# A language-model tower on one core: twelve shared groups ahead of the experts instead of eight, their input read from DRAM, and the own tokens' numbers worked out late

## What is computed

```python
table = where(is_num[:, None], sin(num_value[:, None] / 1000.0 * arange(1, 129)), weight)   # 12500 x 128
h = table[x]                                                  # 128 x 128 tokens, D = 128
# attention: 8 heads of 64, over each sequence; LN is a layer norm without weights
q, k, v = LN(h) @ Wq, LN(h) @ Wkv                              # split into heads
dots = q @ k.T * scale[h]; dots = where(eye, -1e-9, dots)
attn = mix_post(softmax(mix_pre(dots)))                       # 8x8 mixes over the heads
h = h + (attn @ v) @ Wout + bout
# experts: a shared MLP for all tokens, and two banks of 8 experts, top 1, 1280 places each
x2 = LN(h)
y = gelu(x2 @ Ws1 + bs1) @ Ws2 + bs2                          # FF = 512
y = y + bank(x2, Wr_sp, W1_sp, W2_sp) + bank(x2, Wr_fq, W1_fq, W2_fq)
out = h + y
# bank: expert = argmax(softmax(x2 @ Wr + br)); a token beyond place 1280 of its expert adds 0;
#       otherwise gate * (gelu(x2 @ W1[e] + b1[e]) @ W2[e] + b2[e])
```

## Time and profile before

| | |
|---|---|
| median of 3 runs | 1506.09 us (1505.55 to 1506.47) |
| profiled execution: its own time, its span | 1516.0 us, 1514.3 us |
| busy share TensorE, VectorE, ScalarE, GpSimd | 97%, 69%, 76%, 63% |
| mean granted TensorE clock | 0.997 of full speed |
| setup / attention / experts / shared stage, by the trace | 0 to 64.2 / to 1052 / to 1333 / to 1514.3 us |

### The profile page before, as it was taken

How to read it: one execution, slowest core, us unless ns; L and a number is a source line. 1 busy time by engine, 2 the same in 40 slices (tenths; PEclk the granted TensorE clock), 3 DMA queues, 4 the chain that set the end, 5 groups by cost and what they waited for, 6 DMA issues and landing times. The chain is left out here.

```text
span 1514.3 us, 33889 instructions
## 1 busy us (share of the span) xinstructions
PE 1465.3 (97%) x11160; PEld 1339.9 (88%) x11160; DVE 1047.0 (69%) x2811; ACT 1146.8 (76%) x3477; POOL 959.1 (63%) x991
## 2 busy tenths in 40 slices
PE   5789999999999999999999999988999999999999
PEld 2469888888888988889888898877999999999999
DVE  7887788788777887778887787763344333356665
ACT  5589888888888888888888888865555555555555
POOL 7175567888788888788878877664677566510000
PEclk9999999999999999999999999999999999999999
DMA  7324511211211111111111111022244234456665
GB/s 237 132 73 163 164 38 49 69 48 42 60 38 39 55 42 36 35 56 34 36 56 34 37 38 48 26 60 67 69 116 106 70 71 109 120 158 190 189 184 146
DMA packets 171503, 126.48 MB, mean 84 GB/s; under 512 B 30309, under 2 KB 154959, under 8 KB 171330
## 3 DMA queue, kind: packets, MB, share of 16 engines
q1 hardware_dynamic: 153794, 104.15, 23.3%
q0 software_dynamic: 17536, 20.17, 4.8%
HBM read 61.64 MB, written 78.66 MB: 93 GB/s over the span
## 5 line engine op out<-in xcount | busy, mean ns | idle before, releaser
L1129 ACT ACTIVATE expd<-masked,nmax 128x128 f32<-128x128 f32 x1024 | 396.0, 393 | 0.3 <-DVE nmax L1282 0.3
L925 POOL TENSOR_TENSOR prob<-expd,rtotal 128x1024 f32<-128x1024 f32 x128 | 243.5, 1902 | 117.3 <-DVE rtotal L1251 115.8
L1265 DVE COPY_PREDICATED masked<-off_diag,ps_s 128x1024 f32<-128x1024 int32 x128 | 175.0, 1367 | 164.3 <-PE ps_s L1018 164.3
L1062 PE MATMUL ps_o<-u,probT 128*128 128x128 f32 x2048 | 249.0, 275 | 0.0
L1062 PEld LDWEIGHTS ps_o<-u,probT 128*128 128x128 f32 x2048 | 238.9, 191 | 0.0
L1129 ACT ACTIVATION_READ_ACCUMULATOR expd<-masked,nmax 128x1 f32 x1024 | 197.0, 192 | 0.0
L1138 ACT ACTIVATE u<-ps_ut 128x1024 f32<-128x1024 f32 x128 | 131.4, 1026 | 66.3 <-PE ps_ut L1073 66.3
L1227 DVE TENSOR_TENSOR w_lo<-ps_w,w_hi 128x512 fp32r<-128x512 f32 x256 | 164.3, 681 | 0.9 <-ACT w_hi L1167 0.9
L1167 ACT ACTIVATE w_hi<-ps_w 128x512 fp32r<-128x512 f32 x256 | 146.1, 595 | 15.7 <-PE ps_w L1048 9.3
L1158 ACT ACTIVATE probT<-ps_ut 128x1024 f32<-128x1024 f32 x128 | 131.4, 1027 | 33.9 <-PE ps_ut L1030 27.5
L1046 PE MATMUL ps_w<-xT_hi,M_hi 128*128 128x256 f32 x512 | 154.1, 301 | 3.0 <-DVE xT_lo L1221 2.2
(11 more groups left out here) (261 smaller groups left out, 3824.9 us busy)
## 6 DMA issues: line engine op xcount, KB each, us to landing
turned<-x2T SPq DMA_DIRECT2D x32, 256.0 KB, 2.2
answers_sp<-zeros SPq DMA_DIRECT2D x16, 512.0 KB, 4.3
answers_fq<-zeros SPq DMA_DIRECT2D x16, 512.0 KB, 3.8
xT<-turned SPq DMA_DIRECT2D x56, 128.0 KB, 2.3
sh_back<-answers_sp SPq DMA_DIRECT2D x56, 128.0 KB, 2.4
sh_back<-answers_fq SPq DMA_DIRECT2D x56, 128.0 KB, 2.5
out<-res SPq DMA_DIRECT2D x56, 128.0 KB, 2.1
h_sb<-in_L_tok_weight SPq DMA_DIRECT2D x12, 512.0 KB, 5.9
```

The source lines that it names most:

```text
L925: nc.gpsimd.tensor_tensor(prob[k % 2][:, :].rearrange("p (g j) -> p g j", g=H), expd[k % 2][:, :].rearrange("p (g j) -> p g j", g=H), rtot ...
L1062: mm = nc.tensor.matmul(ps_o[:, 0:D], probT[k % 2][:, g * N:(g + 1) * N], u[k % 2][:, g * D:(g + 1) * D], start=(g == 0), stop=(g == H - 1))
L1129: ins = nc.scalar.activation(expd[(k - 1) % 2][:, g * N:(g + 1) * N], masked[(k - 1) % 2][:, g * N:(g + 1) * N], ACT.Exp, bias=nmax[(k - 1 ...
L1265: nc.vector.copy_predicated(masked[k % 2][:, :].rearrange("p (g j) -> p g j", g=H), off_diag[:, :].unsqueeze(1).to_broadcast([P, H, N]), p ...
```

## The change

Setup: VectorE makes all thousandths at once (`slice(0, VS)`) into `part`; `numbers` now holds the plain number and the flag, so that `kept` is written before the weights are loaded, and the own tokens' thousandths are made from the gathered plain numbers behind `reduce(5)`. The turns (`turn_b` and its like) go from VectorE to GpSimd. On GpSimd the own numbers are gathered ahead of the head masks, two and two own rows behind them, and the two fills of `masked` go from ScalarE to GpSimd, behind the products. On TensorE `turn` and `coefficients` come a step later, and `product` n in steps 6 to 12 instead of 5 to 12, two in the last. `WARM` is 6 instead of 13.

Attention: `HEAD` is 12. A group's xT comes by DMA from `turned` into `x1` or `expd[0]` (`load_head`, `head_x`), so `norm2`, `head_norm` and the turn into `ps_w` go; up uses `ps_s` and `ps_w` by turns (`up`); the three schedules are new. Shared stage: 52 groups; the head rows are summed a group of 256 rows at a time, every second step from step 1.

```diff
-HEAD = 8
+HEAD = 12
...
-WARM = 13
+WARM = 6
...
+            link.inc(nc.gpsimd.tensor_scalar(turn_b, row_f[:, :], TURN_HI, 0.0, ALU.mult, ALU.add))
+            link.inc(nc.gpsimd.tensor_scalar(turn_lo, row_f[:, :], TURN_LO, 0.0, ALU.mult, ALU.add))
+            link(nc.gpsimd.tensor_scalar(turn_hi.bitcast(F32R), row_f[:, :], TURN_HI, 0.0, ALU.mult, ALU.add))
+            link(nc.gpsimd.tensor_tensor(turn_b, turn_b, turn_hi, ALU.subtract))
+            link(nc.gpsimd.tensor_tensor(turn_lo, turn_lo, turn_b, ALU.add))
+            link(nc.gpsimd.tensor_tensor(turn_b, turn_hi, turn_lo, ALU.subtract))
+            pool.wait_ge(S["link"], 1)
+            link(nc.gpsimd.tensor_tensor(turn_b, turn_b, is_hi[:, :].to_broadcast([KR, D]), ALU.mult))
+            nc.gpsimd.tensor_tensor(turn_b, turn_b, turn_lo, ALU.add).then_inc(S["turn"], 1)
...
+            pool.wait_ge(S["ids0"], 16)
+            pool.wait_ge(S["kept"], 32)
+            for t in range(OWN):
+                own_number(t)
...
-            pool.wait_ge(S["kept"], 32)
-            for t in range(OWN):
-                own_number(t)
-            pool.wait_ge(S["coef_out"], 2)
-            pool.wait_ge(S["wT_out"], 1)
-            for c in range(2 * HC):
-                mix(c)
+            for t in range(2):
+                own_row(t)
             for t, value in ((C.power, -0.5), (C.ones, 1.0), (C.tri, 1.0), (C.carry, 0.0), (C.chosen, 0.0), (C.var, 1.0)):
                 link.inc(nc.gpsimd.memset(t[:, :], value))
             for m in (*C.mv1, *C.mv2):
                 link.inc(nc.gpsimd.memset(m[:, :, :], 1.0))
             made["mv1"] = link.n
+            for t in range(2, OWN):
+                own_row(t)
+            pool.wait_ge(S["coef_out"], 2)
+            pool.wait_ge(S["wT_out"], 1)
+            for c in range(2 * HC):
+                mix(c)
+            for k in range(2):
+                link.inc(nc.gpsimd.tensor_copy(masked[k][:, :].rearrange("p (g j) -> p g j", g=H),
+                                               diag[:, :].unsqueeze(2).to_broadcast([P, H, N])))
...
+            sp.wait_ge(S["numbers"], 2)
+            sp.dma_start(kept[0:P * VR, :].rearrange("(p r) c -> p (r c)", p=P),
+                         numbers[:, 0:VR, :].rearrange("p r c -> p (r c)")).then_inc(S["kept"], 16)
+            sp.dma_start(kept[P * VR:VOCAB, :], numbers[0:REST, VR, :]).then_inc(S["kept"], 16)
...
-                if 5 <= c:
+                for n in {6: (0,), 7: (1,), 8: (2,), 9: (3,), 10: (4,), 11: (5,), 12: (6, 7)}.get(c, ()):
...
+            link(nc.vector.tensor_copy(numbers[:, 0:VS, 0], num_i[:, :]))
+            thousandths(slice(0, VS), flags=True)
+            halves(slice(0, CHUNKS - 1), VC)
...
+                    thousandths(slice(VS, VX))
...
-        AFTER = {129: (0,), 130: (1,), 131: (2,), 132: (3,), 136: (4,), 138: (5,), 139: range(6, HEAD + 2)}
-        BEHIND = {129: (0,), 130: (1,), 131: (2,), 134: (3,), 137: (4,), 139: range(5, HEAD + 2)}
-        BESIDE = {129: (0,), 131: (1,), 132: (2,), 133: (3,), 136: (4,), 137: (5,), 139: range(6, HEAD + 2)}
-        names = ("head_w", "head_made", "head_turned", "head_xhi", "head_xlo", "head_up", "head_gelu",
+        AFTER = {129: (1,), 130: (2,), 131: (3,), 132: (4,), 135: (5,), 136: (6,), 137: (7,), 139: range(8, HEAD + 2)}
+        BEHIND = {128: (0,), 129: (1,), 130: (2,), 131: (3,), 132: (4,), 135: (5,), 137: (6,), 139: range(7, HEAD + 2)}
+        BESIDE = {128: (0,), 129: (1,), 130: (2,), 131: (3,), 132: (4,), 135: (5,), 136: (6,), 137: (7,), 139: range(8, HEAD + 2)}
...
+        def up(m, f):
+
+            return hidden(ps_s, f) if m % 2 == 0 else ps_w[f // 2][:, f % 2 * GROUP:(f % 2 + 1) * GROUP]
+
+        def head_x(n):
+
+            return expd[0][:, n % 4 * GROUP:(n % 4 + 1) * GROUP] if n % 4 > 1 else x1[n % 4][:, :]
...
+            def load_head(groups):
+                for n in groups:
+                    need(sp, S["head_xlo"], n - 3)
+                    sp.dma_start(head_x(n), turned[n // 2, :, n % 2 * GROUP:(n % 2 + 1) * GROUP]).then_inc(s_head[n % 4], 16)
...
+                        sp.wait_ge(s_kept[k], 16 * (HEAD // 4 + 1))
+                    sp.wait_ge(S["x_turned"], GROUPS)
+                    load_head(range(2))
+                    sp.wait_ge(S["normed"], TILES - 1)
+                    load_head(range(2, 4))
+                if q == QUADS - 2:
+                    load_head(range(4, 8))
+            load_head(range(8, HEAD))
...
-                    if n < HEAD:
-                        pe.wait_ge(S["head_made"], n + 1)
-                        need(pe, S["head_xlo"], n - 1)
-                        need(pe, S["w_lo"], GROUPS * 4)
-                        for b in range(2):
-                            mm = nc.tensor.transpose(ps_w[n % 2][:, b * P:(b + 1) * P], x1[n % 2][:, b * D:(b + 1) * D], ident[:, :])
-                        mm.then_inc(S["head_turned"], 1)
                     if 0 <= n - 1 < HEAD:
                         m = n - 1
                         pe.wait_ge(S["head_xlo"], m + 1)
                         pe.wait_ge(S["copied"], TILES)
-                        need(pe, S["head_gelu"], m)
+                        pe.wait_ge(S["w_lo"], GROUPS * 4)
+                        need(pe, S["head_gelu"], m - 1)
                         for f in range(FC):
-                            h = hidden(ps_s, f)
+                            h = up(m, f)
...
-                        act.wait_ge(S["head_turned"], n + 1)
+                        act.wait_ge(s_head[n % 4], (n // 4 + 1) * 16)
                         need(act, S["head_up"], n - 3)
-                        nc.scalar.activation(xT_hi[:, n % 4, :], ps_w[n % 2][:, 0:GROUP],
+                        nc.scalar.activation(xT_hi[:, n % 4, :], head_x(n),
...
-                        head_norm(0)
                         link.wait()
                         link.inc(nc.vector.tensor_tensor(ws1_lo, ws1, ws1_hi.bitcast(F32), ALU.subtract))
-                    if n + 1 < HEAD:
-                        head_norm(n + 1)
                     if n < HEAD:
                         dve.wait_ge(S["head_xhi"], n + 1)
-                        nc.vector.tensor_tensor(xT_lo[:, n % 4, :], ps_w[n % 2][:, 0:GROUP],
+                        nc.vector.tensor_tensor(xT_lo[:, n % 4, :], head_x(n),
...
-        HEADS_FROM = 4
-
-        def head_tile(i, k):
-
-            n = (k - HEADS_FROM) // 3
-            return (n, n) if (k - HEADS_FROM) % 3 == 0 and 0 <= n < 2 * HEAD else None
+        HEADS_FROM = 1
+
+        def head_group(k):
+
+            n = (k - HEADS_FROM) // 2
+            return n if (k - HEADS_FROM) % 2 == 0 and 0 <= n < HEAD else None
...
+                n = head_group(k + 2)
+                if n is not None:
                     need(sp, S["one_out"], n - 1)
                     for b in range(BANKS):
-                        sp.dma_start(one_back[b][n % 2][:, :], answers[b][bass.ds(t * P, P), :]).then_inc(s_one[n % 2], 16)
...
+                n = head_group(k)
+                if n is not None:
                     dve.wait_ge(s_one[n % 2], (n // 2 + 1) * 32)
+                    need(dve, S["one_out"], n)
+                    for b in range(2):
+                        t = 2 * n + b
+                        ins = nc.vector.scalar_tensor_tensor(one_part[:, b, :], one_back[0][n % 2][:, b, :], gates[:, 2 * t:2 * t + 1],
+                                                             h_sb[:, t * D:(t + 1) * D], ALU.mult, ALU.add)
+                    ins.then_inc(S["one_part"], 1)
+                n = head_group(k - 1)
+                if n is not None:
+                    dve.wait_ge(S["one_part"], n + 1)
                     need(dve, s_one_put[n % 2], n // 2 * 16)
-                    need(dve, S["one_out"], n)
-                    nc.vector.scalar_tensor_tensor(one_part[:, :], one_back[0][n % 2][:, :], gates[:, bass.ds(t * 2, 1)],
-                                                   h_sb[:, bass.ds(t * D, D)], ALU.mult, ALU.add).then_inc(S["one_part"], 1)
-                    dve.wait_ge(S["one_part"], n + 1)
-                    nc.vector.scalar_tensor_tensor(one_out[n % 2][:, :], one_back[1][n % 2][:, :], gates[:, bass.ds(t * 2 + 1, 1)],
-                                                   one_part[:, :], ALU.mult, ALU.add).then_inc(S["one_out"], 1)
+                    for b in range(2):
+                        t = 2 * n + b
+                        ins = nc.vector.scalar_tensor_tensor(one_out[n % 2][:, b, :], one_back[1][n % 2][:, b, :], gates[:, 2 * t + 1:2 * t + 2],
+                                                             one_part[:, b, :], ALU.mult, ALU.add)
+                    ins.then_inc(S["one_out"], 1)
```

(11 more changed lines are left out.)

105 lines of the change are left out of this document (34 added, 71 removed).

## The result

The changed kernel takes 1527.73 us (median of 4 runs, 1524.25 to 1527.98) against 1505.82 us for the kernel before beside it (1504.11 to 1506.47): ratio 1.0142, 95% interval 1.0124 to 1.016. It is 1.4% slower, 12.4 us more than predicted and outside the range. Its profiled execution took 1527.67 us with a span of 1525.9. (One timed execution of the kernel before, beside later runs, took 2663.67 us at a granted clock of 0.76; it is in none of the comparisons.)

What follows compares the result with a forecast made beforehand. It took TensorE, busy 97% of the span, as the bound, and the end of GpSimd's run in the setup. Setup +4.9, tail +15.4, shared -12.6 and +0.5, clock +1: +9.2 on 1506.1, 1515.3 us, range 1502 to 1521.

Steps and rivals of the forecast that it cites:

- from the profiled execution to the median: Last step: the profiled execution lay 9.9 us above the runs' median, 1506.1; that difference was carried over to the forecast.
- (a): Setup: GpSimd's eight products begin at 22 to 25.5 us, taken as 24, so no shift.
- (b): Setup: the two fills of masked on GpSimd behind the products keep VectorE blocked 2.1 us more (0 to 3.8).
- (c): Setup: own numbers worked out behind reduce(5), eight chained operations of 0.19 to 0.2 us; TensorE resumes 1.6 us later.
- (d): Setup: all eight TensorE products now stand behind the wait for the own numbers; one more behind the stall, 1.9 us.
- (e): Setup: WARM 13 to 6 drops 14 matmuls, 1.6 us, of which only 0.65 us comes off.
- Tail: Attention's tail: work +12.1 us, idle 11.2 against 7.9, with waits of 2.3, 2.7, 1.7, 2.8; +15.4 us (11 to 17).
- Shared: Last stage: four fewer groups at 3.16 us, -12.6, and +0.5 for the wait at its start.
- Clock: Tail: gaps of 2.3 to 2.8 us may lower the granted clock, 0 to 5 us; +1 taken.
- the second place would fill the gaps: Rival: tail idle falls to 3.5 us, products begin 1.5 us sooner, fills and numbers find cover; 1499.7 us, chance 0.15.
- one had the tail filled too: Rival: the tail fills but the setup loses; +0.5, 1506.6 us, chance 0.13.
- the other the setup even: Rival: tail as walked, fills don't block VectorE and products begin early; +4.3, 1510.4 us, chance 0.15.

Runs made afterwards that it cites:

- gather_ahead: The kernel before with the last of GpSimd's four own-number gathers moved behind the products' two waits, directly ahead of the products; 1516.67 us, 1.0076.
- setup_only: The kernel before with the changed kernel's setup and WARM 6; 1522.25 us, 1.0117.
- fills_act: setup_only with the two fills of masked back on ScalarE; 1522.06 us, 1.0121.
- copy_first: setup_only with a GpSimd wait for the fourth reduction added ahead of its products, which had nothing to wait for; 1523.39 us, 1.012.
- both: The changed kernel with the wait of copy_first and the four tail steps moved as in tail_order; 1515.67 us, 1.0072.
- early_only: setup_only with VectorE's small operations on the own numbers moved ahead of the products, no idle added; 1517.68 us, 1.0093.
- tail_order: tail_only with four tail steps moved: gelu(0) and gelu(1) later, down(2)'s sum behind the normalizing, xT_lo(7) ahead of the last router step; 1497.43 us, 0.9952.
- tail_only: The changed kernel with the setup of the kernel before and WARM 13; 1509.88 us, 1.0042.
- mixes_late: The kernel before with a GpSimd wait for ScalarE's third sine added ahead of its eight products; 1506.4 us, 1.0009.
- rows_first: Changed setup on the old tail and stages, GpSimd's four row gathers ahead of its wait for kept, own numbers early; 1505.46 us, 1.0013.
- best: The changed kernel with the setup of rows_first and the tail of tail_order; 1496.5 us, 0.9955.
- memset_ahead: The kernel before with six memsets moved from behind GpSimd's products to directly ahead of them, behind their waits; 1504.19 us, 1.0003.
- idle_ahead: setup_only with a GpSimd wait for ScalarE's copy of wkT added ahead of the products, leaving idle time there; 1519.5 us, 1.0091.
- tail_act: tail_only with only ScalarE's part of the reordering, gelu(0) behind u(126) and gelu(1) behind u(127); 1503.19 us, 0.9983.

## Why the prediction was wrong

- **The step that failed is the last one: from the profiled execution to the median.** "That execution is 9.9 us above the median of the runs; the difference goes to the median." It took the 9.9 us as an offset that every profiled execution has over the runs. They were a thing in that one profile: the lock-out of VectorE, which gather_ahead prices at 11.5 us. Most executions of the kernel before don't have it; the changed setup has it in all six profiles in which its gathers of rows stand directly ahead of the products (after, setup_only, fills_act, copy_first, both, early_only). So the earlier trace rows, on which the setup was priced, is not the course that the median of before goes: against the usual course the setup costs 17.1 us (setup_only), not 4.9. Against the profile the forecast was +9.2 (1525.2 us), and 1527.67 was measured: 2.5 us off. The other 9.9 us of the miss are this step. The prediction had the number in hand (an execution 0.66% over runs that agreed within 0.06%) and the row (a copy of 15.58 us where its neighbours take 1.29) and didn't join them.
- **The 2.5 us are in part luck.** Against the profile of the rows the first turn came 5.9 us later (4.9 predicted). Behind it stand 1.8 us more until the first scores and 1.3 in the attention loop (922.2 us against 920.9), both priced at nothing, and the tail's 16.6 (15.4, and 1 for the clock). The experts, priced at nothing too, took 2.2 us less: their first 20 us had a granted clock of 0.83 before and 1.00 after, which is 3.4 us, while the wait for their rows was 1.2 us instead of 0.6. That gain, which no term foresaw, covers about half of what the setup, the start and the loop cost beyond the forecast.
- **(a) Products at 24.** They began at 25.57, 1.6 us late and 0.07 past the bounds of 22 to 25.5. `kept` landed at 11.45 and not by 10.5, and a mask on GpSimd took 1.52 us against a copy. More important than when: what stands ahead of them. That was on no list.
- **(b) Fills.** 2.01 us for two, and VectorE was held for both, as said. The Trainium skill ("SBUF — State Buffer", section "Who interferes with whom"), by which a GpSimd instruction that reads blocks a two-input VectorE instruction, agrees: 17.94 us with the fills (setup_only), 15.97 without (fills_act).
- **(c), (d), (e).** From the end of the fills to TensorE's resumption 4.67 us (47.06 less 42.39), where before had 3.33: +1.3 against 1.6. From there to the first turn 23.75 against 22.8: +0.95 against 1.9 - 0.65 = 1.25. All right in the locked course. In the other course (c) is 14.8 us, and the prediction had no rival for it.
- **Tail.** The four waits came as walked: 2.31, 2.66, 1.54 and 2.56 against 2.3, 2.7, 1.7 and 2.8. From last scores to last down +16.6 us against +15.4 (75.5 less 58.9); the clock was 0.91 from 1025 to 1045 us in it, so the +1 for the clock belongs here.
- **Shared.** From its first matmul to the end 169.4 us against 181.3: -11.9, predicted -12.1.
- **Clock.** +1 was taken for the tail. tail_order shows 3.7 beyond the waits (12.5 less 8.8), and the attention's start lost 1.8 us more than in the profile of before (9.0 us from first turn to first scores, against 7.2; clock 0.66 from 70 to 80 us). In after's own tail the clock was 0.96 over the first 38 us, 1.5 us lost, with the same waits that came with 5.0 in tail_only.
- **Rivals.** That the second place would fill the gaps fell, since they are the order of the program, and for the reason given; moving four steps fills most of them. The other two fell as well: one had the tail filled too, the other the setup even, and it costs 5.9 us even against the locked course.

## What to carry to other kernels

Where the profiled execution lies apart from the timed ones by more than they lie apart from each other, look for the rows that make it so before anything is priced: here the offset was a course that the other runs don't take. Two waits that end together hide each other: the table above has 2.8 and 4.6 us for either and 17.5 for both, so a cause is not cleared because its removal alone brings little. In a chain of engines near its end, give each engine what another waits for ahead of what fills (u before gelu, the normalizing before a sum), and count the cover of the longest latency (router to rows) in units of work before moving any away.

## What the runs showed of the hardware

- GpSimd's eight products and VectorE's two-input copies take turns, product by product (20.2 us for eight instead of 14.86, a copy 1.3 to 3.0), or GpSimd keeps VectorE out for the whole run, 15.6 to 17.9 us. Eight profiles are of the locked kind (before's of the rows, after, setup_only, fills_act, copy_first, both, gather_ahead, early_only): in each the products follow a gather on GpSimd within 0.04 us and begin before VectorE's copy. In the other twelve either a copy was under way when the products began, or (mixes_late, rows_first, best) GpSimd had idled over 2 us. So a gather made to stand directly ahead brings the lock (gather_ahead), and 2.4 us of idle at the same place don't. Whether it must be a gather, or any busy GpSimd does it when no copy is under way, is open: memset_ahead began during a copy. So is a shorter idle time without a copy under way, and why the lock comes at all.
- The Trainium skill ("SBUF — State Buffer", section "Who interferes with whom") says that whoever issues first gets the pair for the whole instruction. Per instruction mixes_late agrees (the copy waits 1.4 us for one product and then runs); it doesn't say that the lock can outlast the instruction, and the earlier trace rows and gather_ahead show VectorE out for eight of them.
- While turns are taken, a VectorE operation on 128x4 elements takes 1.82 us instead of 0.17 (idle_ahead), one product per operation, whether it has two inputs from SBUF (L645) or one (L644).
- Six waits of 0.9 to 2.7 us on TensorE within 55 us (tail_only) came with 10 us at the 1.2 GHz level in 80 us. The same waits cost less in after (0.96 over 38 us, else 1.00). Without the two of 2.3 and 2.7 us (tail_act), and without the four largest (tail_order), the clock was 1.00.
